# Banded attention masks: written into the four PSUM banks by ScalarE instead of by TensorE matmuls, with a new order of the steps

## The reference, cut to what matters

```python
mask = (j > i) & (j <= i + W)            # W = 64: a band of 64 keys behind each query
sc = jnp.where(mask, einsum(Qb, Kw) / sqrt(D), -jnp.inf)
p = softmax(sc); local = einsum(p, Vw)
lmask = arange(N_LATENTS)[None, :] <= (arange(Sx) // chunk)[:, None]
lsc = jnp.where(lmask, einsum(GQ, GK) / sqrt(LAT_HD), -jnp.inf)   # 64 pooled keys
lp = softmax(lsc); rem = einsum(lp, GV)
```

## Time and profile before

| | |
|---|---|
| time, median of 3 runs | 1186.57 us (1186.52 to 1190.21) |
| time of the profiled execution | 1185.35 us, its span 1183.5 us |
| TensorE (PE) busy | 1120.4 us, 95% |
| VectorE (DVE) busy | 863.6 us, 73% |
| ScalarE (ACT) busy | 677.8 us, 57% |
| GpSimd (POOL) busy | 240.9 us, 20% |
| mean granted TensorE clock | 0.991 of full |
| TensorE's share of the chain that ended last | 74% (ACT 9%, DVE 9%, issue 4%) |

### The profile page before, as it was taken

One profiled execution on the slowest core, in us unless ns is written; L12 is line 12 of the kernel. 1 busy time (PEld: TensorE's weight loads), 2 busy tenths in 40 slices (PEclk: granted clock), 3 DMA queues, 4 the chain that ended last, 5 costly groups with the idle time before them and its releaser, 6 DMA issues.

```text
span 1183.5 us, 32775 instructions
## 1 busy us (share of the span) xinstructions
PE 1120.4 (95%) x13168; PEld 804.7 (68%) x13168; DVE 863.6 (73%) x3425; ACT 677.8 (57%) x1415; POOL 240.9 (20%) x336
## 2 busy tenths in 40 slices
PE   6878979999999999999999999999999999998998
PEld 3545545676677677777777677777777777776776
DVE  6898968978878887869676885877477895653333
ACT  1677757567755756575665746557474744443231
POOL 2222022042112230221203220122203220210111
PEclk9989979999999999999999999999999999999999
DMA  9510100001000001010000101000001000000000
GB/s 332 147 48 15 37 16 16 25 26 45 25 16 29 28 3 55 2 42 29 29 15 5 44 2 34 15 21 15 11 12 34 15 17 19 3 20 20 3 19 19
DMA packets 27353, 38.59 MB, mean 33 GB/s; under 512 B 3536, under 2 KB 21328, under 8 KB 27200
## 3 DMA queue, kind: packets, MB, share of 16 engines
q1 hardware_dynamic: 25296, 34.29, 9.0%
q10 hardware_dynamic: 1904, 2.20, 0.6%
HBM read 31.79 MB, written 4.29 MB: 30 GB/s over the span
## 4 chain that ended last, share of the span: by engine, by line
PE 74%; ACT 9%; DVE 9%; issue 4%; POOL 3%; DMA 1%; ACTq 0%; DVEq 0%; POOLq 0%
PE psg L455 45%; PE psq L455 17%; PE pso L455 7%; PE psg L458 6%; ACT PQ L1450 3%; POOL M L1797 2%; ACT M L1450 1%; DVE nm L992 1%; DMA QK<-in_w 1%; ACT JA L1461 1%; DVE JD L1005 1%; DVE R L989 1%; ACT QK L1450 1%; POOL R L1822 1%; DVE sf L989 0%
## 5 line engine op out<-in xcount | busy, mean ns | idle before, releaser
L1450 ACT ACTIVATE PQ<-psq 128x2048 f32<-128x2048 f32 x112 | 210.2, 1876 | 66.2 <-PE psq L455 65.7
L1822 POOL TENSOR_TENSOR R<-R,rhoT 128x256 f32<-128x256 f32 x128 | 92.7, 746 | 424.3 <-ACT R L1450 424.3
L455 PE MATMUL psq<-QK 32*128 32x128 f32 (+5 forms) x3360 | 128.1, 302 | 1.8 <-DMA QK<-in_w 1.8
L455 PE MATMUL psg<-zT,WiT 128*128 128x256 f32 x480 | 114.5, 381 | 2.1 <-DVE R L989 1.9
L455 PEld LDWEIGHTS psq<-QK 32*128 32x128 f32 (+2 forms) x3360 | 97.0, 165 | 25.7 <-issue 18.3
L455 PE MATMUL pso<-PQ,Vg 128*32 128x256 f32 (+2 forms) x2048 | 109.4, 345 | 4.5 <-ACT PQ L1450 2.4
L455 PE MATMUL psg<-WoT,R 128*128 128x256 f32 x480 | 107.9, 380 | 0.0
L992 DVE TENSOR_REDUCE nm<-psq 128x16 f32<-128x2048 f32 (+1 forms) x48 | 92.8, 1933 | 20.5 <-PE psq L455 19.8
L1450 ACT ACTIVATE R<-psg 128x512 f32<-128x512 f32 x60 | 35.7, 595 | 113.5 <-PE psg L455 113.2
L455 PEld LDWEIGHTS psg<-WoT,R 128*128 128x128 f32 x480 | 89.3, 190 | 13.1 <-issue 1.2
L455 PEld LDWEIGHTS psg<-zT,WiT 128*128 128x128 f32 x480 | 86.9, 190 | 15.4 <-DVE R L989 2.6
(11 more groups left out here) (236 smaller groups left out, 2272.8 us busy)
## 6 DMA issues: line engine op xcount, KB each, us to landing
bcB<-ada_rows SPq DMA_DIRECT2D x16, 384.0 KB, 3.4
bcA<-ada_rows SPq DMA_DIRECT2D x15, 384.0 KB, 3.3
X<-in_x SPq DMA_DIRECT2D x16, 256.0 KB, 3.0
XR<-in_x SPq DMA_DIRECT2D x16, 256.0 KB, 2.7
out<-XR SPq DMA_DIRECT2D x15, 256.0 KB, 2.1
QK<-NMT SPq DMA_DIRECT2D x96, 4.0 KB
WiT<-in_WiT SPq DMA_DIRECT2D x1, 1024.0 KB, 5.1
WoT<-in_WoT SPq DMA_DIRECT2D x1, 1024.0 KB, 7.7
```

Source lines behind the costliest of these rows:

```text
L455: return e.matmul(o, lhsT, rhs, start=start, stop=stop, skip_group_check=True)
L1450: return e.activation(o, i, func, **kw)
L1822: e.tensor_tensor(R4, R4, rhoT[:, :], ALU.mult).then_inc(*pool_moe.mark(b, f"r{f}{j}"))
```

## The change

No mask goes through TensorE any more. `tiles` and `unit` are gone. `maskb` holds each mask at full width (1408 columns instead of 1016), and ScalarE copies it into all four banks with one activation instruction for each filling: three new steps of a ScalarE stage `maxi`, three new steps in its stage `loc`. The copy waits until the banks have been emptied; the scores wait for the copy. On TensorE a step without instructions, `reserve`, fixes the place of the filling in the row of fillings. In `att`, `start` of the second half is now `kt == 0`, so that the flags which make a matmul add are left as the copies need them; the number of matmuls there stays. GpSimd prepares `maskb` with seven small copies in place of one. The `ORDER` strings of all five engines are new, apart from their beginnings.

```diff
+            def reserve(key, end):
+                emptied[key] = quad.take(key, end)[1]
...
             def maxi(b):
                 qk = QK2[b % 2]
                 yield
-                take(quad, ("a", b), dve_max.at(b, "a"))
-                if not b:
-                    w.wait_ge(*pool_late.at(0, "mask"))
                 w.wait_ge(*act_proj.at(b, "gk1"))
-                for i, j, r, o in tiles():
-                    mm(psq[o, i, :].rearrange("p (r n) -> p r n", r=4), unit(r),
-                       MQ[r, 96 - 32 * j:224 - 32 * j].unsqueeze(1).broadcast_to([32, 4, 128]), True, False)
+                reserve(("a", b), dve_max.at(b, "a"))
+                yield
+                w.wait_ge(*act_max.at(b, "a"))
                 for ek in range(4):
...
             def loc(b):
+                def turn(v):
+                    reserve(("lc", b, v), act_loc.at(b, f"p{v}"))
+
                 def scores(v):
                     pslot["p2", b, v] = pq.take(("p2", b, v), pe_loc.at(b, "pv1" if v else "pv0"))
-                    take(quad, ("lc", b, v), act_loc.at(b, f"p{v}"))
-                    n = 128 if v == 1 else 192
-                    for i, j, r, o in tiles():
...
+                    w.wait_ge(*act_loc.at(b, f"m{v}"))
...
+            def fill(key, o, i, done):
+                w.wait_ge(*pool_late.at(0, "mask"))
+                w.wait_ge(*emptied[key])
+                copy(o, i).then_inc(*done)
+
+            def maxi(b):
+                for m in "ab":
+                    yield
+                    fill((m, b), psq.rearrange("p i (r n) -> p (i r) n", r=4), MAX[m].unsqueeze(1).broadcast_to([128, 16, 128]),
+                         act_max.mark(b, m))
+                yield
+                fill(("l", b), psq[:, :, 0:256].rearrange("p i (e n) -> p i e n", e=2),
+                     MAX["l"].unsqueeze(1).unsqueeze(1).broadcast_to([128, 4, 2, 128]), act_max.mark(b, "l"))
+
             def loc(b):
...
+                def masks(v):
+                    fill(("lc", b, v), psq[:, :, :], TURN[v].unsqueeze(1).broadcast_to([128, 4, 512]), s.mark(b, f"m{v}"))
+
+                yield
+                masks(0)
                 yield
                 exps(0)
                 yield
+                masks(1)
+                yield
                 exps(1)
+                yield
+                masks(2)
```

More of the change, by code:

```diff
@@ L206, in program @@
         identb = sb("identb", [128, 128], BF16)
-        maskb = sb("maskb", [128, 1016], BF16)
+        maskb = sb("maskb", [128, 1408], BF16)
         hsel = sb("hsel", [128, 8])
@@ L321, in program @@
         w2sq = wj[:, 1536:2048].rearrange("p (c n) -> p c n", c=2)
-        MQ, MK, ML, MLT = maskb[:, 0:224], maskb[:, 224:512], maskb[:, 512:632], maskb[:, 632:1016]
+        TURN = maskb[:, 0:512], maskb[:, 512:1024], maskb[:, 0:512]
+        MAX = {m: maskb[:, 1024 + 128 * n:1152 + 128 * n] for n, m in enumerate("abl")}
         nmv = nm.rearrange("p t (e j i) -> p t i e j", e=2, j=3)
@@ L471, in turn4 @@
                 return last
-            def tiles():
-                for i in range(4):
-                    for j in range(4):
-                        yield i, j, slice(32 * i, 32 * i + 32), slice(32 * j, 32 * j + 32)
-            def unit(r):
-                return identb[r, r]
+            def reserve(key, end):
+                emptied[key] = quad.take(key, end)[1]
             def first(b, *names):
@@ L715, in maxi @@
                 yield
-                take(quad, ("b", b), dve_max.at(b, "b"))
-                for i, j, r, o in tiles():
-                    m = 32 - 32 * (j % 2)
-                    mm(psq[o, i, :].rearrange("p (r n) -> p r n", r=4), unit(r),
-                       MQ[r, m:m + 128].unsqueeze(1).broadcast_to([32, 4, 128]), True, False)
+                reserve(("b", b), dve_max.at(b, "b"))
+                yield
+                w.wait_ge(*act_max.at(b, "b"))
                 for ek in range(4):
@@ L730, in maxi @@
                 yield
-                take(quad, ("l", b), dve_max.at(b, "l"))
-                for t in range(2):
-                    for i, j, r, o in tiles():
-                        m = 56 - 32 * t - 8 * j
-                        mm(psq[o, i, 0:256].rearrange("p (e t n) -> p e t n", e=2, t=2)[:, :, t, :], unit(r),
-                           ML[r, m:m + 64].unsqueeze(1).broadcast_to([32, 2, 64]), t == 0, False)
+                reserve(("l", b), dve_max.at(b, "l"))
+                yield
+                w.wait_ge(*act_max.at(b, "l"))
                 for ee in range(2):
@@ L1755, in _ @@
             in_order(ORDER["ACT"], late=late, prep=prep, norm=norm, qkv=qkv, heads=heads, att=att, outp=outp, fin=fin, norm2=norm2,
-                     fin2=fin2, proj=proj, loc=loc, mix=mix, moe=moe)
+                     fin2=fin2, proj=proj, maxi=maxi, loc=loc, mix=mix, moe=moe)
         @block.gpsimd
@@ L1776, in late @@
                 w.wait_ge(*loads["mf"])
-                e.tensor_copy(maskb[:, :], mf).then_inc(*pool_late.mark(0, "mask"))
+                for o, i, n in ((0, 0, 192), (192, 0, 192), (384, 0, 128), (512, 0, 128), (640, 0, 128), (768, 192, 256), (1024, 448, 384)):
+                    last = e.tensor_copy(maskb[:, o:o + n], mf[:, i:i + n])
+                last.then_inc(*pool_late.mark(0, "mask"))
                 w.wait_ge(*loads["wgkv"])
@@ L1864, in late @@
                 yield
-                load(e, "mf", mf, A["masks"])
+                load(e, "mf", mf[:, 0:832], A["masks"])
                 load(e, "wat0", wat[:, :, 0:768], chunks("wat")[:, :, 0:768])
@@ L1960, in allow @@
         return np.where(m, np.float32(0), neg).astype(np.float32)
-    p = q[:, None] % 32
-    cols = lambda n, first: np.arange(n)[None] - first
-    m_q = allow((p - cols(224, 96) >= 0) & (p - cols(224, 96) < 64))
-    m_k = allow((cols(288, 96) - p >= 0) & (cols(288, 96) - p < 64))
-    m_l = allow(cols(120, 56) <= p // 4)
-    m_t = allow(p <= cols(384, 128) // 4)
+    p = q[:, None]
+    cols = lambda n: np.arange(n)[None]
+    m_k = allow((cols(192) >= p) & (cols(192) - p < 64))
+    m_t = allow(p % 64 <= cols(256) // 4)
+    m_a = allow((p >= cols(128)) & (p - cols(128) < 64))
+    m_b = allow((p % 64 + 64 >= cols(128)) & (p % 64 + 64 - cols(128) < 64))
+    m_l = np.concatenate([allow(cols(64) <= (p + 128 * t) // 4) for t in range(2)], axis=1)
     hs = np.zeros((128, 8), np.float32)
@@ L1985, in _inputs @@
     return {
[L1986 removed]
+        "x": f("x"), "condT": np.pad(T_(f("cond_1024")), ((0, 0), (0, 16))), "ident": np.eye(128, dtype=np.float32), "masks": cat(m_k, m_t, m_a, m_b, m_l),
         "hsel": hs, "sidx": np.array([1.0, 0.0], np.float32), "ltm": ltm,
```

137 lines of the change are left out of this document (68 added, 69 removed).

## The result

The changed kernel took **1279.59 us** (median of 4 runs, 1272.81 to 1282.29) against 1187.12 for the kernel before in the same runs: a ratio of 1.077 (95% interval 1.074 to 1.080), 92.5 us slower. The forecast was 1182 us, the range 1164 to 1200.

A forecast was written before the change was run, and what follows sets the result against it. TensorE was taken to bound the kernel (busy 1120.4 of 1183.5 us), the chain of the four banks being second. 1185.35 - 33.8 + 28 - 3.5 + 4 = 1180.1, plus 1.2 for the median, rounded up to 1182 us; range 1164 to 1200.

The forecast's parts named there:

- the rounding up from 1181.3 to 1182: Whole kernel: last step of the sum, an allowance for what the new order may have put elsewhere.
- What waits behind the copies: ScalarE's in-order row: copies hold small copies and ReLUs TensorE needs; its other middle idling, 8.0 us, grows 1.5-fold, 4 us more.
- waits on other ScalarE results grown by over 10 us: Sign of a wrong prediction: TensorE's waits for ReLU and small copies grow this much, making the kernel slower.
- The load rule: ScalarE, middle: load rises from 0.60 to 0.74, not the bound by its sum; other waits grow as queueing does, by 1.5.
- Removed: 33.8 us: TensorE: start-to-start distances of all 96 mask blocks (80 of about 0.37 us, 16 of about 0.27), all that it saves.
- Bank waits: +28 less 3.5: Four banks `psq`: the copy lengthens the chain, 45 us of waits, 28 more; 3.5 counted as hidden in the first 200 us.
- the factor 0.76: Bank waits seen in the trace before (16.7 us) against those worked out (22.1), applied to the new order's 59.2 us.
- the table: Missing TensorE work between bank fillings in three stretches: before 15.1, 4.1, 2.9 us; after 24.2, 17.6, 17.4.
- the single place: Batch 14, `b` to `l`: 0.88 us of work where 3.61 are needed, so TensorE stands 2.7 us.
- The method of missing work: All 159 pairs of successive bank fillings: TensorE work between them against the chain's need; missing 22.1 us before, 59.2 after.
- ScalarE's busy time: Whole kernel: 96 copies (80 of 1.88 us, 16 of 1.02) add 167 us, from 678 to about 845 us, 71%.
- ScalarE's queue decides: Rival, about 1198 us: copies hold what TensorE waits for, 1.88 us each; clock stretches 3.4 us each at both ends; chance 0.28.

The follow-up runs named there:

- f3: Kernel before, old order, mask matmuls left out with nothing in their place, so scores overwrite the banks: 1169.23 us, ratio 0.9841.
- e2: Changed kernel with all 96 copies and their waits, each writing 16 columns of each bank instead of 512, nearly all masks left out: 1256.59 us, ratio 1.0568.
- g3: Changed kernel plus 273 idle matmuls ahead of 61 TensorE steps where the trace shows it idle: 1259.07 us, ratio 1.0598.
- g4: Kernel before plus 96 idle matmuls ahead of 27 TensorE steps: 1183.78 us, ratio 0.996.
- f1: Kernel before, its orders kept, with all 96 masks copied by ScalarE instead of matmuls: 1299.66 us, ratio 1.0936.
- e1: Changed kernel's new order on all engines, all masks by matmul again, ScalarE's copies and their waits gone: 1277.68 us, ratio 1.0747.
- g2: f2 with its 28 copies cut to 16 columns a bank, waits kept, those blocks' masks left out: 1185.99 us, ratio 0.9986.
- g1: Kernel before, masks by matmul, with five SBUF-to-SBUF copies on ScalarE at each of f2's 28 places, which no engine waits for: 1214.22 us, ratio 1.021.
- f2: Kernel before, old order, with only 28 masks copied by ScalarE (`a` and some of turn 0), the others by matmul: 1224.16 us, ratio 1.0307.

## Why the prediction was wrong

**The account of the 92.5 us**, from whole kernels: the mask matmuls gone, -18 us (f3 against before); the new order, +87.4 (e2 against f3, 1256.59 - 1169.23, both without mask matmuls or full copies); the copies in that order, +23.0 (changed kernel against e2). Together 92.4. Of this loss the low clock holds about 16: idle matmuls won back 20.5 us in the changed kernel (g3) and 4.1 in the kernel before (g4).

This is one of two ways from the one kernel to the other, and the parts depend on the way. All six kernels:

| | no full masks | masks by matmul | copies |
|---|---|---|---|
| old order | 1169.23 (f3) | 1187.12 (before) | 1299.66 (f1) |
| new order | 1256.59 (e2) | 1277.68 (e1) | 1279.59 (changed) |

With copies in place the new order is 20 us *faster* than the old one. It does what it was made for: copies cost 23 us in it and 130 in the old one. But it is some 90 us slower wherever no long copies stand in ScalarE's row, and with copies neither order comes near the kernel before. So "the order costs 90 us" holds for kernels without full copies; what is shown for the change is that neither the copies in the old order nor the new order by itself is cheap.

**The step that failed** is the cost of the new order outside the four banks. The sum has two terms for it: the rounding up from 1181.3 to 1182 "for what the new order may have put elsewhere", 0.7 us without any working, and the 4 us of "What waits behind the copies". The latter took the 8.0 us that TensorE idled for other things in the middle and scaled them by ScalarE's load, which assumes that apart from the banks the new order feeds TensorE as well as the old one did. It doesn't: e1, with no copy in it, idles 50.8 us in the middle against 11.1, and takes 89.8 us more. What remains, the exchange of matmuls for copies within the new order, was forecast at -33.8 + 28 - 3.5 + 4 = -5.3 us and measured at +1.9 (changed kernel against e1), no change clear of the noise. The prediction had the order of both kernels and went through it pair by pair, but only for fillings of the four banks; for all other results (`R`, `rho`, `zT`, `OO`, the exponentials that `pso` waits for) it never asked how long after its producer a step stands. More than half of the growth is waits for VectorE, which no term priced. The prediction did name, as a sign that it was wrong, waits on other ScalarE results grown by over 10 us: they grew by 19. The cost of the order lies there and in the low clock that follows the gaps (the profiled e1 is 96.2 us longer than the profiled kernel before: 57.4 us more idle outside the banks, 2.8 more at them, and 36.0 more busy at a clock of 0.967), and TensorE at 98.6% in the middle can't make up for any of it.

**The load rule was wrong in kind.** Busy share says little of an in-order queue in which results are just in time. f1 and g2 put 0.80 to 0.85 us of time on each us of ScalarE work in the old order, at 57% to 65% busy; g1, without any bank, 0.63. In the new order the price was 0.17 (e2). So the load alone doesn't set the price. To put 0.63 on each of the 156 us that ScalarE got gives 98 us, near the 92.5 by chance alone, since e1 loses 89.8 us without that work.

**Removed: 33.8 us, measured 18.** The distances were read rightly: in f3 TensorE is busy 30.3 us less (1090.1 against 1120.4). But it idles 12.1 us more (75.2 against 63.1), as f3's expectation said: what it waits for doesn't come earlier by as much. At the banks, for one, its waits for VectorE's maxima are 5.6 us where the same view of before has 2.7.

**Bank waits: +28 less 3.5, measured +26.3.** Right, and in its parts: with the factor 0.76 the table gives 18.4, 13.4 and 13.2 us, and in the stretches ahead of 222 us, up to 1036 and behind it the trace has 16.3, 13.2 and 13.9. At the single place TensorE waits 1.68 us at the bank and 2.4 in all, where 2.7 were worked out. The method of missing work held here, for a chain whose every link is in the count; it fails when the cost lies in another engine's row, as f1 showed (its time grew by 112 us where the count gave 10).

**ScalarE's busy time** (845 forecast, 833.6 measured) and the price of a copy (1.88, 1.881) were right. **TensorE busy** was forecast at 1086 and is 1135.7. Some 44 of these 50 us are the low clock (55 us not granted against 11), which the sum had at nothing.

**The rival "ScalarE's queue decides"** named queue and clock and was the nearest in number, yet at 1198 far too small, and with the copies as the cause, which e1 does without. It counted nine copies that hold something up, and clock stretches only "at both ends". The earlier trace rows showed the price; what was missing was that idling all over the middle brings them there too.

The Trainium skill (ScalarE: Activation LUTs, "Step-by-step: what each stage is for") has ScalarE faster into PSUM than into SBUF. The longest rows can't tell, since each has PSUM at one end: 2048 elements take 1881 ns from SBUF into PSUM (`psq<-maskb`) and 1876 ns from PSUM into SBUF. With SBUF as the source the runs lean to the page's side, by little: 256 elements into SBUF take 409 ns (g1), and a straight line between the copies into PSUM of 64 elements (226 ns, e2) and of 1024 (1024 ns) would put 256 at about 386 ns, an estimate.

The Trainium skill (TensorE: Matmul & The Clock Gate, "What's actually happening") says that the low clock is the state at rest and activity lifts it. g3 and g4 agree: idle matmuls alone took the mean granted clock from 0.957 to 0.997 and from 0.991 to 0.999.

**What stays open.** Which engine's row of the new order costs most. The five orders depend on each other, and no run exchanges one alone; e1 shows only that the five together cost about 90 us. That steps stand too close behind their producers is read from where TensorE waits in e1; no run moved such steps apart. The split of f2's cost between queue and bank chain is worked out from g1, whose dummy work was shorter than f2's copies. The expectation of g2 held (1183 to 1195 us), and those of g3 (1235 to 1260) and g4 (1175 to 1184) only just. The 87.4 us of the order hold the slivers' own 226 ns and their waits for emptied banks; e1 against before, without them, gives 89.8.

## What to carry to other kernels

Before moving work from the bound engine to one that is "only" 57% busy, ask what stands behind it in that engine's queue: put dummy work of that length at those places and time it (g1 is ten lines), rather than reading the busy share. When a change brings a new order of everything, measure the order by itself first (e1: new order, old work) and the work by itself (f1: old order, new work), since their costs need not add up; and when reading the order, hold every producer against its consumer, not only those of the resource that the change is about. And once the bound engine idles in many short gaps, count its clock as well as the gaps.

## What the runs showed of the hardware that was not expected

The clock can be bought back with idle matmuls: 96 of them at 27 places made the kernel before 4.1 us (0.4%) faster, whatever they delayed included. Each us of clock won back was worth less than a us of time, 0.40 us (g3) and 0.43 us (g4).

Copies of 128x256 that follow each other on ScalarE overlap: 140 of a mean of 409 ns made 45.7 us of busy time, not 57.

Work put into ScalarE's row in the old order cost 0.63 us of time for each us though nobody waited for its result (g1), at 57% busy.
